# A split-fp16 product transposed by DMA in place of TensorE, and loops written out, in a gated two-layer kernel

## The chip, the cores and the metric

The kernel runs on one core of a Trainium2 chip. The metric is the device time of one execution in microseconds (us); the text compares medians of several runs. The profile is one execution, recorded by the hardware profiler. Engines are named as in the profile: PE is TensorE's matrix multiply, PEld its weight load, DVE is VectorE, ACT is ScalarE, POOL is GpSimd, SP is SyncE, which here only issues DMAs.

## The reference

There are 2048 tokens `x` of 512 numbers. Two layers follow each other. The first sends each token through the expert that its token id names (four experts, each one 512x512 matrix `W`, used for all three products of the layer); the second is a low-rank mixture of eight experts, of which each token takes its best two:

```python
# layer 1, per token with its expert e (Wg = Wu = Wd = ctx_2048):
h  = layernorm(x)
g  = silu(h @ Wg[e].T);  u = h @ Wu[e].T
x  = x + tanh(g_xattn) * ((g * u) @ Wd[e].T)
# layer 2, E = 8 experts of rank R = 16, top K = 2:
h2 = layernorm(x)
gates = softmax(h2 @ Wr + br + bonus);  top2 = top_k(gates, 2)
hid = relu(h2 @ Wd + bd);  eo = hid @ Wu + bu
x  = x + tanh(g_ffn) * sum_e(weight_e * eo_e)
```

Since `Wg` is `Wu`, the kernel computes one product `a` and forms `silu(a) * a` from it.

## The kernel before

**Tiles and pairs.** The tokens are sorted by expert, by gathers, into 16 tiles of 128 tokens. A tile that holds tokens of two experts is worked on once for each, so there are 19 (tile, expert) pairs. One step `i` of the program works on several pairs at once, as a software pipeline; each engine has its own list of instructions in an order written out by hand, and semaphores join them.

**Split products.** Each fp32 factor is split into two fp16 numbers, a high part and a low part, and a product is three matmuls (high by high, high by low, low by high) for each of four 128-deep slices: 12 matmuls (`split_product`, L603 to L605).

**A pair's way.** For pair `k`: ACT normalizes the tile (`h`, L824), PE transposes it (`ps_hT`), ACT and DVE split that into `hT_hi` (L810) and `hT_lo` (L1074), PE forms the first product `ps_a`, ACT takes `silu` (L805), DVE forms `prod` (L1068). In the next step PE transposes `prod` (four 128x128 fp32 transposes into PSUM, `ps_pT`, L624), ACT copies the high part `pT_hi` (L783), DVE subtracts it and leaves the low part `pT_lo` (L1104), PE forms the second product `ps_y`, and DVE adds it to the tile (L1086).

**A tile's way in layer 2.** When all pairs of a tile are added, DVE takes statistics (L1095, L1099), POOL the reciprocal root (`ve`, `rs`, `mrs`, L456 to L458), ACT normalizes (`h`, L796), PE transposes (`ps_h2T`, L685), ACT and DVE split (`h2T_hi` L815, `h2T_lo` L1110), PE forms the gates and hidden values (`ps_hid`), DVE finds the best two, ACT takes their `tanh` (`half_tanh`, L801), DVE forms the weights (`w`, L1169) and the weighted hidden values, PE transposes those (`ps_wT`) and forms the low-rank product (`ps_o`), and DVE adds it (L1117). POOL scatters the finished tile to its place.

**Order on the engines.** In a steady step DVE runs: best two, `wtT_lo`, `gwT`, `pT_lo` of the pair before, `w` and the weighting, `prod`, `hT_lo`, `h2T_lo`, the addition of the low-rank product, the addition of the second product of the pair before, statistics, hidden values. ACT runs: `pT_hi`, `wtT_hi`, `gwT`, `h` of layer 2, `tanh`, `silu`, `hT_hi`, `h2T_hi`, `h` of layer 1 for the pair after the next. PE runs: the hidden product, the four transposes of `prod`, the first product, the low-rank product, the transposes of `h`, those of layer 2's `h`, the second product of the pair before, the transposes of the weights.

**Start.** In the first steps ACT also squares and converts the expert weights and those of layer 2 (`square_sums`, `high_parts`, `ffn_squares`, L740 to L766), between the parts of the steps.

**Loops.** `pipeline` joins steps that do the same work into a loop whose body holds two steps: PE for steps 8 to 17, ACT for 8 to 13 and 15 to 16, DVE for 9 to 12 and 14 to 17. Step 13 is written out on DVE and POOL's work is written out throughout. In a loop the index is in a register; DVE clears a cell (`gate`, L1049) ahead of some instructions there, which takes their waits. SP counts arrived gathers into one semaphore (`x_in`), which a loop can wait for.

## Time and profile before

| what | value |
|---|---|
| median of 3 runs | 203.54 us (202.56 to 203.68) |
| span of the profiled execution | 201.4 us |
| busy on PE, share of the span | 175.0 us, 87% |
| busy on DVE | 155.7 us, 77% |
| busy on ACT | 111.9 us, 56% |
| busy on POOL | 99.7 us, 50% |
| mean DMA rate over the span | 67 GB/s |

The profiled execution's own time is its span, 201.4 us, and what lies around it; the median of the runs is 2.1 us above the span. Busy shares are means over the whole program, in which the start (weights are loaded, squared, split and transposed), the steady steps, and the end differ. A steady step takes a little over 8 us, and its limits are read from the timeline of each engine, not from the shares. A time ahead of an instruction's name is its start, counted from the span's start; the number behind it is its duration; instructions of one engine are pipelined, so the next one can start before the duration is over.

### The profile page before, as it was taken

The page shows a single profiled execution, that of the slowest core. Times are in us where ns is not written, and L with a number is a line of the kernel's source. Part 1 is how long each engine was busy: PE and PEld are TensorE (multiplying, and loading weights), DVE is VectorE, ACT ScalarE, POOL GpSimd, SP SyncE. Part 2 cuts the span into 40 slices and gives each one's busy share as a digit, 9 for nine tenths or more (in the row PEclk, how much of TensorE's full clock was granted, in tenths as well). Part 3 has the DMA queues.
Part 4 walks back from the last instruction along what each step waited for, and adds up shares of the span by engine and source line. Part 5 has one row for each costly group of instructions (what it writes and reads, how often), then busy time and mean ns, then how long its engine had stood idle before and what let it go on. Part 6 is the DMA issues. An engine that isn't in the chain of part 4 may idle for free.

```text
span 201.4 us, 4382 instructions
## 1 busy us (share of the span) xinstructions
PE 175.0 (87%) x1074; PEld 104.0 (52%) x1075; DVE 155.7 (77%) x523; ACT 111.9 (56%) x224; POOL 99.7 (50%) x246
## 2 busy tenths in 40 slices
PE   1576896999997989999999999999999999976560
PEld 1564463655553656656656556655665655534310
DVE  4859696697768799889888998797877878678640
ACT  2596599884287166473665726547265561545200
POOL 4478846427246366375553735516244162445641
PEclk9999999999999999999999999999999999999955
DMA  5947572101210201203101011011010100101121
GB/s 135 370 163 231 205 216 69 52 5 20 86 55 0 52 0 52 59 0 104 55 0 54 0 52 52 2 52 52 0 54 0 52 20 33 52 0 55 52 104 52
DMA packets 6784, 13.43 MB, mean 67 GB/s; under 512 B 2392, under 2 KB 2520, under 8 KB 6768
## 3 DMA queue, kind: packets, MB, share of 16 engines
q0 software_dynamic: 2560, 8.39, 12.6%
q1 hardware_dynamic: 4208, 4.86, 7.3%
q8 instruction: 6, 0.10, 0.2%
q14 instruction: 10, 0.08, 0.2%
HBM read 9.06 MB, written 4.19 MB: 66 GB/s over the span
## 4 chain that ended last, share of the span: by engine, by line
PE 44%; issue 18%; POOL 10%; DVE 9%; DMA 7%; ACT 4%; DVEq 3%; SPq 2%; POOLq 1%; ACTq 0%
PE ps_y L603 6%; PE ps_y L605 6%; PE ps_y L604 6%; PE ps_a L603 4%; PE ps_a L605 4%; PE ps_a L604 4%; DMA xs<-in_x_dram,rows_of 4%; ACT h L796 3%; POOL rs L457 3%; PE ps_h2T L685 2%; PE ps_pT L624 2%; DMA bu_nat<-in_L_ffn_bu_dram 2%; POOL hot_slot L432 2%; PE ps_hT L677 2%; POOL xs L439 2%
## 5 line engine op out<-in xcount | busy, mean ns | idle before, releaser
L456 POOL TENSOR_SCALAR ve<-mv 128x1 f32<-128x1 f32 x32 | 7.7, 239 | 62.6 <-DVE mv L1099 51.8
L796 ACT ACTIVATE h<-xs,mrs,rs 128x512 f32<-128x512 f32 (+1 forms) x16 | 21.1, 1317 | 22.4 <-POOL mrs L458 22.4
L783 ACT ACTIVATE pT_hi<-ps_pT 128x512 f16<-128x512 f32 x19 | 11.3, 595 | 36.0 <-PE ps_pT L624 36.0
L603 PE MATMUL ps_y<-w_hi,pT_hi 128*128 x76 | 28.8, 379 | 2.3 <-DVE w_lo L952 1.5
L603 PE MATMUL ps_a<-w_hi,hT_hi 128*128 x76 | 29.1, 382 | 0.7 <-DVE hT_lo L1074 0.6
L604 PE MATMUL ps_a<-w_lo,hT_hi 128*128 x76 | 29.1, 382 | 0.0
L605 PE MATMUL ps_a<-w_hi,hT_lo 128*128 x76 | 29.0, 381 | 0.0
L604 PE MATMUL ps_y<-w_lo,pT_hi 128*128 x76 | 28.8, 379 | 0.0
L605 PE MATMUL ps_y<-w_hi,pT_lo 128*128 x76 | 28.8, 379 | 0.0
L1086 DVE SCALAR_TENSOR_TENSOR xs<-ps_y,y_t,xs 128x512 f32 x19 | 14.3, 750 | 10.2 <-PE ps_y L605 7.7
L529 POOL DMA_INDIRECT out_dram<-xs,rows_of x16 | 17.3, 1083 | 5.9 <-DVE xs L1117 3.5
L457 POOL TENSOR_TENSOR rs<-ve,neg_half 128x1 f32<-128x1 f32 x32 | 18.9, 592 | 2.7
L439 POOL DMA_INDIRECT xs<-in_x_dram,rows_of x16 | 17.0, 1064 | 3.7 <-issue 2.9
L824 ACT ACTIVATE h<-xs,mrs,rs 128x512 f32 (+1 forms) x19 | 15.6, 820 | 4.3 <-POOL mrs L458 3.8
L1068 DVE SCALAR_TENSOR_TENSOR prod<-ps_a,prod_bits,silu 128x512 f32<-128x512 f32 x19 | 14.1, 744 | 1.6 <-ACT silu L805 1.6
L805 ACT ACTIVATE silu<-ps_a,inv_bits 128x512 f32<-128x512 f32 x19 | 12.8, 676 | 4.2 <-PE ps_a L605 4.2
L685 PE MATMUL ps_h2T<-ident,h 128*128 128x128 f32 x64 | 10.2, 281 | 4.2 <-ACT h L796 4.1
L1104 DVE TENSOR_TENSOR pT_lo<-ps_pT,pT_hi 128x512 f16<-128x512 f32 x19 | 13.1, 689 | 0.7 <-ACT pT_hi L783 0.3
L1117 DVE SCALAR_TENSOR_TENSOR xs<-ps_o,out_coef,xs 128x512 f32<-128x512 f32 (+1 forms) x16 | 11.9, 742 | 2.0 <-PE ps_o L645 2.0
L1074 DVE TENSOR_TENSOR hT_lo<-ps_hT,hT_hi 128x512 f16<-128x512 f32 x19 | 12.9, 680 | 0.3 <-ACT hT_hi L810 0.3
L740 ACT ACTIVATE sq_act<-w_nat 128x512 f32<-128x512 f32 x16 | 10.1, 634 | 5.4 <-DMA w_nat<-in_ctx_dram 5.0
L632 PE MATMUL ps_hid<-w_in_hi,h2T_hi 128*128 128x136 f16 x64 | 12.1, 223 | 0.6 <-DVE h2T_lo L1110 0.4
(209 smaller groups left out, 424.0 us busy)
## 6 DMA issues: line engine op xcount, KB each, us to landing
w_nat<-in_ctx_dram SPq DMA_DIRECT2D x4, 1024.0 KB, 7.9
xs<-in_x_dram,rows_of POOLq DMA_INDIRECT x16, 3.6
wd_nat<-in_L_ffn_Wd_dram SPq DMA_DIRECT2D x1, 256.0 KB
wu_nat<-in_L_ffn_Wu_dram SPq DMA_DIRECT2D x1, 256.0 KB
out_dram<-xs,rows_of POOLq DMA_INDIRECT x16, 2.9
...
tok_i<-in_itok_BxS_dram SPq DMA_DIRECT2D x1, 8.0 KB, 1.8
```

The lines of the kernel that those rows point to most:

```text
L439: g.indirect_dma_start(out=xs[:, t, :], out_offset=None, in_=x_rows[:, :], in_offset=bass.IndirectOffsetOnAxis(ap=rows_of[:, t:t + 1], axi ...
L457: then(g.tensor_tensor(rs[:, n, k:k + 1], ve[:, n, k:k + 1], neg_half[:, :], ALU.pow))
L529: g.indirect_dma_start(out=out_rows[:, :], out_offset=bass.IndirectOffsetOnAxis(ap=rows_of[:, k:k + 1], axis=0), in_=x1[:, k, :], in_offse ...
L603: mm(ps[:, :], lhs_hi[:, kc, :], hi, start=(kc == 0), stop=False)
L604: mm(ps[:, :], lhs_hi[:, kc, :], lo, start=False, stop=False)
L605: last = mm(ps[:, :], lhs_lo[:, kc, :], hi, start=False, stop=(kc == KC - 1))
L685: last = tr(ps_h2T[:, c, :], h2[:, c, :], ident[:, :])
L796: a(h2[:, :, :], x1[:, col(k), :].rearrange("p o (q c) -> p c (o q)", c=KC), ACT.Identity, bias=mrs[:, 1, col(k)], scale=rs[:, 1, col(k)]) ...
L824: a(h[:, :], flat(xs[:, col(tile), :]), ACT.Identity, bias=mrs[:, 0, col(tile)], scale=rs[:, 0, col(tile)]).then_inc(normed1, 1)
L1068: v.scalar_tensor_tensor(prod[:, :], ps_a[:, :], prod_t[:, col(k)], silu[:, :], ALU.mult, ALU.mult).then_inc(prod_done, 1)
L1086: v.scalar_tensor_tensor(flat(x1[:, col(tile), :]), ps_y[:, :], y_t[:, col(k)], flat(xs[:, col(source), :]), ALU.mult, ALU.add).then_inc(x ...
L1104: v.tensor_tensor(pT_lo[:, :, :], ps_pT[:, :, :], pT_hi[:, :, :], ALU.subtract).then_inc(pT_lo_done, 1)
```

## The change

PE no longer transposes `prod`. ACT copies `prod`'s high part (`p_hi`, from SBUF) and DVE subtracts it and leaves the low part (`p_low`), both side by side in a tile `p_split` with two buffers; SP issues one DMA per pair that transposes the two parts (128 x 1024 fp16 numbers, 256 KB) into `pT`, also of two buffers. The second product waits for that DMA. `p_hi` of pair `i` stands on ACT behind `h2T_hi` and ahead of layer 1's `h`, and `p_low` of pair `i` on DVE behind `h2T_lo` and ahead of the addition of the low-rank product, both in step `i`, where `pT_hi` and `pT_lo` of pair `i` stood in step `i + 1`. All loops are written out; `gate` and `x_in` are gone.

```diff
-                sp.sem_inc(x_in, 1)
...
+            for k in range(NP):
+                sp.wait_ge(p_hi_done, k + 1)
+                sp.wait_ge(p_lo_done, k + 1)
+                if k >= 2:
+                    sp.wait_ge(y_done, k - 1)
+                sp.dma_start_transpose(pT[:, k % 2, :, :, :].rearrange("p s c q -> p (s c) q"),
+                                       p_split[:, k % 2, :, :].rearrange("p s d -> p (s d)"))\
+                  .then_inc(pT_in[k % 2], 16)
             sp.wait_ge(s_scatter, 16 * T)
...
             def second_product(k, e):
-                pe.wait_ge(pT_lo_done, k + 1)
+                pe.wait_ge(pT_in[k % 2], 16 * (k // 2 + 1))
...
-                split_product(ps_y, pT_hi, pT_lo, e).then_inc(y_done, 1)
-
-            def transpose_product(k):
-
-                pe.wait_ge(prod_done, k + 1)
-                for c in range(KC):
-                    last = tr(ps_pT[:, c, :], prod[:, c * P:(c + 1) * P], ident[:, :])
-                last.then_inc(pT_done, 1)
+                split_product(ps_y, pT[:, k % 2, 0, :, :], pT[:, k % 2, 1, :, :], e).then_inc(y_done, 1)
...
@@ ACT, step @@
-                if some(NP, -1, i0):
-                    k = i - 1
-                    act.wait_ge(pT_done, k + 1)
-                    wait_last(act, y_done, k)
-                    a(pT_hi[:, :, :], ps_pT[:, :, :], ACT.Copy).then_inc(pT_hi_done, 1)
...
+                if some(NP, 0, i0):
+                    k = i
+                    act.wait_ge(prod_done, k + 1)
+                    if k >= 2:
+                        act.wait_ge(pT_in[k % 2], 16 * (k // 2))
+                    a(p_split[:, k % 2, 0, :], prod[:, :], ACT.Copy).then_inc(p_hi_done, 1)
...
@@ DVE @@
             def product(k):
                 dve.wait_ge(silu_done, k + 1)
+                wait_last(dve, p_lo_done, k)
...
-            def pT_low(k):
-
-                dve.wait_ge(pT_hi_done, k + 1)
-                v.tensor_tensor(pT_lo[:, :, :], ps_pT[:, :, :], pT_hi[:, :, :],
-                                ALU.subtract).then_inc(pT_lo_done, 1)
+            def p_low(k):
+
+                dve.wait_ge(p_hi_done, k + 1)
+                if k >= 2:
+                    dve.wait_ge(pT_in[k % 2], 16 * (k // 2))
+                v.tensor_tensor(p_split[:, k % 2, 1, :], prod[:, :], p_split[:, k % 2, 0, :],
+                                ALU.subtract).then_inc(p_lo_done, 1)
...
-                if some(NP, -1, i0) and not ending:
-                    pT_low(i - 1)
...
                 if some(T, -2 - LATE, i0) and not draining:
                     h2T_low(i - 2 - LATE)
+                if some(NP, 0, i0):
+                    p_low(i)
                 if some(T, -4 - LATE, i0) and not draining:
                     add_low_rank(i - 4 - LATE)
...
-        def pipeline(eng, step, first, pairs, tiles):
...
-                    with eng.Fori(0, (last - first) // 2) as n:
-                        step(n * 2 + (first + odd), first)
-                        step(n * 2 + (first + odd + 1), first)
...
+        def pipeline(step, first, pairs, tiles):
+
+            for i in range(first, max(NP - min(pairs), T - min(tiles))):
+                step(i, i)
```

On DVE, in a full step that is written out before (`xs` in the last row is the addition of the low-rank product), the program before has:

```order
L1150 TENSOR_TENSOR wtT_lo<-ps_wT,wtT_hi 128x128 [waits wtT_hi_done]
L1151 TENSOR_TENSOR gwT<-ps_wT,gwT 8x128
L1104 TENSOR_TENSOR pT_lo<-ps_pT,pT_hi 128x512 [waits pT_hi_done]
L1169 SCALAR_TENSOR_TENSOR w<-half_dif,half_tanh,half_sum 128x8 [waits wtT_done,mix_done,tanh_done]
L1172 SCALAR_TENSOR_TENSOR weighted<-hid,w 128x128 [waits w8_done]
L1176 TENSOR_SCALAR w_rep<-w,ffn_bits 128x3x8
L1068 SCALAR_TENSOR_TENSOR prod<-ps_a,prod_bits,silu 128x512 [waits silu_done]
L1074 TENSOR_TENSOR hT_lo<-ps_hT,hT_hi 128x512 [waits hT_hi_done]
L1110 TENSOR_TENSOR h2T_lo<-ps_h2T,h2T_hi 128x512 [waits h2T_hi_done]
L1117 SCALAR_TENSOR_TENSOR xs<-ps_o,out_coef,xs 128x512 [waits o_mm]
```

The changed program has there (`p_split` is written by `p_low`; its lines are numbered anew):

```order
L1115 TENSOR_TENSOR wtT_lo<-ps_wT,wtT_hi 128x128 [waits wtT_hi_done]
L1116 TENSOR_TENSOR gwT<-ps_wT,gwT 8x128
L1132 SCALAR_TENSOR_TENSOR w<-half_dif,half_tanh,half_sum 128x8 [waits wtT_done,mix_done,tanh_done]
L1135 SCALAR_TENSOR_TENSOR weighted<-hid,w 128x128 [waits w8_done]
L1139 TENSOR_SCALAR w_rep<-w,ffn_bits 128x3x8
L1035 SCALAR_TENSOR_TENSOR prod<-ps_a,prod_bits,silu 128x512 [waits p_lo_done,silu_done]
L1041 TENSOR_TENSOR hT_lo<-ps_hT,hT_hi 128x512 [waits hT_hi_done]
L1077 TENSOR_TENSOR h2T_lo<-ps_h2T,h2T_hi 128x512 [waits h2T_hi_done]
L1071 TENSOR_TENSOR p_split<-prod,p_split 128x512 [waits pT_in0,p_hi_done]
L1084 SCALAR_TENSOR_TENSOR xs<-ps_o,out_coef,xs 128x512 [waits o_mm]
```

The subtraction for the low part moved from ahead of `w`, for the pair before, to behind `h2T_lo`, for the pair of this step.

On ACT, at the start of the program, after the first product of pair 1, the program before has (the row of `h` is layer 1's for tile 3, then come the squares of the weights; `pT_hi` of pair 1 follows behind all squares):

```order
L805 ACTIVATE silu<-ps_a,inv_bits 128x512 [waits a_done]
L810 ACTIVATE hT_hi<-ps_hT 128x512 [waits a_done,hT_done]
L820 TENSOR_LOAD pair_tile_i
L820 ISA x2
L824 ISA [waits hT_done,rstd1]
L824 ACTIVATE h<-xs,mrs,rs 128x512
L740 ACTIVATE sq_act,row_sq<-w_nat 128x512 [waits s_sq,s_wload3]
```

The changed program has there:

```order
L774 ACTIVATE silu<-ps_a,inv_bits 128x512 [waits a_done]
L779 ACTIVATE hT_hi<-ps_hT 128x512 [waits a_done,hT_done]
L790 ACTIVATE p_split<-prod 128x512 [waits prod_done]
L795 TENSOR_LOAD pair_tile_i
L795 ISA x2
L799 ISA [waits hT_done,rstd1]
L799 ACTIVATE h<-xs,mrs,rs 128x512
L714 ACTIVATE sq_act,row_sq<-w_nat 128x512 [waits s_sq,s_wload3]
```

The copy of the high part, which waits for `prod` of pair 1, stands ahead of `h` and of the squares, and there is none behind the squares.

## Rows read from the trace of the kernel before

**Rows 1.** Windows: us, busy of PE, PEld, DVE, ACT, POOL, PEclk, DMA share, GB/s

```profile
83.87:92.16 8.29, 8.29 (x58) 5.00 (x55) 7.43 (x26) 4.73 (x9) 5.40 (x13) 1.00 0.14 42
...
134.70:168.22 33.52, 33.49 (x219) 19.98 (x217) 26.50 (x84) 18.24 (x35) 13.29 (x36) 1.00 0.08 32
```

**Rows 2.** Timeline of PE: start us, us, line, operation [idle before, releaser]

```profile
72.06 0.38 PE L603 MATMUL ps_y<-w_hi,pT_hi 128*128 x1
...
75.58 0.60 PE L624 MATMUL ps_pT<-ident,prod 128*128 128x128 f32 x4
76.02 0.38 PE L603 MATMUL ps_a<-w_hi,hT_hi 128*128 x1
...
168.22 0.60 PE L624 MATMUL ps_pT<-ident,prod 128*128 128x128 f32 x4
```

**Rows 3.** Timeline of DVE, the written-out step 13

```profile
130.55 0.23 DVE L1169 SCALAR_TENSOR_TENSOR w<-half_dif,half_tanh,half_sum 128x8 f32<-128x8 f32 x1 [1.19 <-ACT half_tanh L801]
...
131.17 0.73 DVE L1068 SCALAR_TENSOR_TENSOR prod<-ps_a,prod_bits,silu 128x512 f32<-128x512 f32 x1
...
132.42 0.68 DVE L1110 TENSOR_TENSOR h2T_lo<-ps_h2T,h2T_hi 128x512 f16<-128x512 f32 x1
133.02 0.74 DVE L1117 SCALAR_TENSOR_TENSOR xs<-ps_o,out_coef,xs 128x512 f32<-128x512 f32 x1
133.94 0.75 DVE L1086 SCALAR_TENSOR_TENSOR xs<-ps_y,y_t,xs 128x512 f32 x1 [0.18 <-issue]
...
136.99 0.69 DVE L1104 TENSOR_TENSOR pT_lo<-ps_pT,pT_hi 128x512 f16<-128x512 f32 x1
138.60 0.23 DVE L1169 SCALAR_TENSOR_TENSOR w<-half_dif,half_tanh,half_sum 128x8 f32<-128x8 f32 x1 [0.91 <-ACT half_tanh L801]
```

**Rows 4.** Timeline of ACT, the same step

```profile
131.47 0.59 ACT L815 ACTIVATE h2T_hi<-ps_h2T 128x512 f16<-128x512 f32 x1
...
137.06 1.32 ACT L796 ACTIVATE h<-xs,mrs,rs 128x512 f32<-128x512 f32 x1 [0.79 <-POOL mrs L458]
```

**Rows 5.** Timeline of DVE, two additions of the second product

```profile
75.08 0.75 DVE L1086 SCALAR_TENSOR_TENSOR xs<-ps_y,y_t,xs 128x512 f32 x1 [0.29 <-PE ps_y L605]
...
142.52 0.75 DVE L1086 SCALAR_TENSOR_TENSOR xs<-ps_y,y_t,xs 128x512 f32 x1 [0.62 <-PE ps_y L605]
```

**Rows 6.** Timeline of DVE, a subtraction with both inputs in SBUF

```profile
68.54 0.74 DVE L1041 SCALAR_TENSOR_TENSOR wu_lo<-wu_nat,ffn_bits,wu_hi 128x512 f16<-128x512 f32 x1
```

**Rows 7.** Costliest groups: busy us, mean ns of one | idle before, releaser

```profile
L740 ACT ACTIVATE sq_act<-w_nat 128x512 f32<-128x512 f32 x16 | 10.1, 634 | 5.4 <-DMA w_nat<-in_ctx_dram 5.0
```

**Rows 8.** DMA issues: KB each, median us from issue to landing

```profile
w_nat<-in_ctx_dram SPq DMA_DIRECT2D x4, 1024.0 KB, 7.9
xs<-in_x_dram,rows_of POOLq DMA_INDIRECT x16, 3.6
...
tok_i<-in_itok_BxS_dram SPq DMA_DIRECT2D x1, 8.0 KB, 1.8
```

**Rows 9.** Timelines of ACT and DVE at the start, in order of time

```profile
34.08 0.86 ACT L824 ACTIVATE h<-xs,mrs,rs 128x512 f32 x1
...
35.42 0.72 DVE L1068 SCALAR_TENSOR_TENSOR prod<-ps_a,prod_bits,silu 128x512 f32<-128x512 f32 x1
...
39.83 0.60 ACT L783 ACTIVATE pT_hi<-ps_pT 128x512 f16<-128x512 f32 x1 [0.42 <-PE ps_pT L624]
40.32 0.68 ACT L752 ACTIVATE w_hi<-ps_h2T,scale_w 128x512 f16<-128x512 f32 x1
...
44.73 0.75 DVE L1068 SCALAR_TENSOR_TENSOR prod<-ps_a,prod_bits,silu 128x512 f32<-128x512 f32 x1 [0.20 <-ACT silu L805]
```

**Rows 10.** Timelines of PE and DVE, second product of pairs 2 and 18, `prod` of 18

```profile
49.37 0.38 PE L603 MATMUL ps_y<-w_hi,pT_hi 128*128 x1
...
173.43 0.73 DVE L1068 SCALAR_TENSOR_TENSOR prod<-ps_a,prod_bits,silu 128x512 f32<-128x512 f32 x1
...
178.05 0.39 PE L603 MATMUL ps_y<-w_hi,pT_hi 128*128 x1 [0.79 <-DVE pT_lo L1104]
```

More of the change, by code:

```diff
@@ L192, in bass_flamingo_gated_kernel @@
         prod = sb("prod", [P, D])
-        pT_hi = sb("pT_hi", [P, KC, P], fp16)
-        pT_lo = sb("pT_lo", [P, KC, P], fp16)
+        p_split = sb("p_split", [P, 2, 2, D], fp16)
+        pT = sb("pT", [P, 2, 2, KC, P], fp16)
         h2 = sb("h2", [P, KC, P])
@@ L275, in bass_flamingo_gated_kernel @@
         prod_done = sem("prod_done")
[L276 to L278 removed]
+        p_hi_done = sem("p_hi_done")
+        p_lo_done = sem("p_lo_done")
+        pT_in = [sem("pT_in0"), sem("pT_in1")]
         y_done = sem("y_done")
@@ L311, in some @@
             return 0 <= i + off < n
-        def pipeline(eng, step, first, pairs, tiles):
-            def work(i):
-                return ([(some(NP, off, i), i + off == 0) for off in pairs]
-                        + [(some(T, off, i), i + off == 0) for off in tiles])
-            end = max(NP - min(pairs), T - min(tiles))
-            while first < end:
-                last = first + 1
-                while last < end and work(last) == work(first):
-                    last += 1
-                if last == first + 1:
-                    step(first, first)
-                else:
-                    odd = (last - first) % 2
-                    if odd:
-                        step(first, first)
-                    with eng.Fori(0, (last - first) // 2) as n:
-                        step(n * 2 + (first + odd), first)
-                        step(n * 2 + (first + odd + 1), first)
-                first = last
+        def pipeline(step, first, pairs, tiles):
+            for i in range(first, max(NP - min(pairs), T - min(tiles))):
+                step(i, i)
         def col(k):
@@ new lines, in _ @@
+            sp.wait_ge(s_gather[0], 16)
+            load_weights(3)
+            sp.wait_ge(s_gather[1], 16)
+            sp.dma_start(gates_in[:, 0:1], g_xattn.rearrange("(a n) -> a n", a=1).to_broadcast([P, 1])).then_inc(s_gates_in, 16)
+            sp.dma_start(gates_in[:, 1:2], g_ffn.rearrange("(a n) -> a n", a=1).to_broadcast([P, 1])).then_inc(s_gates_in, 16)
+            sp.wait_ge(s_gather[AHEAD - 1], 16)
+            sp.dma_start(b_in[:, 0:ER], bd.rearrange("(a e) r -> a (e r)", a=1).to_broadcast([P, ER])).then_inc(s_small, 16)
@@ new lines, in _ @@
+            sp.dma_start(b_in[:, ER:HC], br.rearrange("(a e) -> a e", a=1).to_broadcast([P, EF])).then_inc(s_small, 16)
+            sp.dma_start(wr_nat[:, :, :], Wr.rearrange("(p c) e -> p c e", c=KC)).then_inc(s_small, 16)
+            sp.dma_start(wd_nat[:, :, :, :], Wd.rearrange("e (p c) r -> p e (c r)", c=KC)).then_inc(s_small, 16)
+            sp.dma_start(wu_nat[:, :], Wu.rearrange("e r d -> (e r) d")).then_inc(s_small, 16)
+            sp.wait_ge(s_const, 2)
+            for n in range(3):
+                sp.dma_start(bu_nat[n * Q:n * Q + EF, :], bu[:, :]).then_inc(s_small, 16)
@@ L727, in _ @@
             pe.wait_ge(s_ffn_w, 2)
-            pipeline(pe, step, 7, (-1, 0, 1), (-2 - LATE, -3 - LATE, -4 - LATE))
+            pipeline(step, 7, (-1, 0, 1), (-2 - LATE, -3 - LATE, -4 - LATE))
         @block.scalar
@@ L856, in _ @@
             ffn_high_parts()
-            pipeline(act, step, 5, (-1, 0, 1, 2), (2, -2 - LATE, -3 - LATE, -4 - LATE))
+            pipeline(step, 5, (-1, 0, 1, 2), (2, -2 - LATE, -3 - LATE, -4 - LATE))
         @block.vector
@@ L1217, in _ @@
             hT_low(1)
+            p_low(0)
             statistics1(3)
@@ L1235, in _ @@
             ffn_out_low_parts()
-            pipeline(dve, step, 6, (-1, 0, 1), (3, -1 - LATE, -2 - LATE, -3 - LATE, -4 - LATE))
+            pipeline(step, 6, (-1, 0, 1), (3, -1 - LATE, -2 - LATE, -3 - LATE, -4 - LATE))
 _INS = ['x', 'itok_BxS_13_99985', 'ctx_2048', 'g_xattn', 'g_ffn', 'L0_ffn_Wr', 'L0_ffn_br',
```

38 lines of the change are left out of this document (1 added, 37 removed).

## The prediction

> **What bounds the kernel now.** I read four views in this order: the window table, the timeline of VectorE over one step, the timelines of ScalarE and TensorE beside it, and the start and end of the program.
>
> The window table shows that TensorE has no gap in the middle of the program: 8.29 us busy in a window of 8.29 us, which is one step, and 33.49 of 33.52 us over four later ones [rows 1]. The granted clock there is 1.00, which is the 2.4 GHz level. Four transposes of `prod` stand in each step: they begin at 75.58 and the next product begins at 76.02, so they cost 0.44 us of TensorE's step [rows 2]. From the first of these (75.58) to the last one in the steady part (168.22) there are 11 steps, 92.64 us, or 8.42 us each.
>
> VectorE's timeline shows a second loop that is as long. In the one steady step whose instructions are written out already (step 13), the operation `w` begins at 130.55 and again at 138.60: 8.05 us [rows 3]. Between them follow, without idle time, `prod`, `hT_lo`, `h2T_lo`, the addition of the low-rank product (L1117), the addition of the second product (L1086) and the statistics. These release GpSimd's reciprocal root, which releases ScalarE's `h` at 137.06; the `tanh` stands behind `h` on ScalarE, and `w` waits for that `tanh` (idle 1.19 us before the first `w`, 0.91 us before the second) [rows 3, 4]. So a microsecond put anywhere between `w` and the statistics comes out at the next `w`. A microsecond put between the statistics and the next `w` doesn't: VectorE idles there anyway. `pT_lo` stands just there, at 136.99, before that idle time. Two loops thus bind at once, TensorE's 8.29 and this one's 8.05 and more; the looped steps are longer than either number because each waits for the other now and then, as the addition that waited 0.62 us for `ps_y` at 142.52 [rows 5].
>
> **The change, part by part.**
>
> *TensorE* loses the four transposes: 8.29 − 0.44 = 7.85 us a step. Alone this pays only as far as the other loop lets it.
>
> *VectorE* does as many subtractions as before, but `p_low` moves from the covered place (136.99) to the place between `h2T_lo` and the addition of the low-rank product, that is between 132.42 and 133.02, inside the chain. A subtraction of this size takes 0.60 us from start to start where its first input lies in PSUM (`h2T_lo`, 132.42 to 133.02) [rows 3]; the nearest row with both tensor inputs in SBUF took 0.74 us (`wu_lo`) [rows 6]. I take 0.65, nearer to the first since it is the same operation. The loop becomes 8.05 + 0.60 to 8.05 + 0.74, that is 8.65 to 8.79; I take 8.70, above TensorE's 7.85, so this loop sets the step. Over 11 steps: 95.7 − 92.6 = **+3.1 us**. In the two steps ahead of that stretch VectorE still waits for `ps_y` (0.29 us at 75.08 [rows 5]), and 0.60 − 0.29 = **+0.3 us** is left.
>
> *ScalarE* copies `p_hi` from SBUF in place of `pT_hi` from PSUM: 0.63 us by the squares of the same size from SBUF [rows 7]. In a steady step `prod` ends at 131.90, so `p_hi` would run from there to 132.53, after `h2T_hi` (begun 131.47, 0.59 us), and be done before `p_low` gets its turn at 133.02 [rows 3, 4]: cost nothing, hidden beside `hT_lo` and `h2T_lo`. If `prod` came later against these two, `p_low` would wait for it and the step would grow by that much.
>
> *The transfer.* One DMA per pair moves 256 KB from SBUF to SBUF and transposes it. No row of before shows such a transfer. Its landing is bounded by 1.8 us (an 8 KB load on the same queue) and 7.9 us (1 MB on the same queue); the nearest row in size is the gather of 256 KB, 3.6 us [rows 8]. I take 3.6. Below 1.8 nothing speaks for it, since that is the least that this queue shows for a far smaller load. In a steady step there is room: from `w` to `p_low`'s end 133.02 − 130.55 + 0.70 = 3.17; then the landing; from the first matmul of the second product to its addition 75.08 − 72.06 = 3.02 [rows 2, 5]; from that addition to the next `w` 138.60 − 133.94 = 4.66 [rows 3]. Together 10.85 us plus the landing have to fit in two steps, 17.4 us: hidden up to a landing of 6.5 us. Beyond, a step is half of the sum, 0.5 us more for each us.
>
> The Trainium skill gives prices for this transfer. "DMA: Bandwidth & Descriptors", section "Latency and other measured facts", has 261 GB/s for a transposing DMA and about 2 us of fixed cost: 1.0 + 2.0 = 3.0 us (estimate), inside the room worked out above. No run here shows it yet.
>
> *The start.* There no low-rank product fills the steps yet, and ScalarE, which squares and converts the weights, is the narrow place. `p_hi` of pair 1 stands ahead of the first normalization of tile 3 (L824), which began at 34.08; but `prod` of pair 1 ends only at 35.42 + 0.72 = 36.14 [rows 9]. That normalization can begin at 36.14 + 0.63 = 36.77, 2.7 us later. Of this, `pT_hi` and its wait go (0.42 idle and 0.49 to the next start, at 39.83), so `w_hi` of 40.32 is 1.8 late. `prod` of pair 2 (44.73) can be late by 0 to 1.8; I take 1.1, as ScalarE has some idle time between: 45.83. Then 0.75 + 0.63 + 0.69 to the end of `p_low` and 3.6 to land: 51.5, where the second product began at 49.37 [rows 10]; +2.1. TensorE works 0.44 less behind it: **+1.7 us**.
>
> *The end.* `prod` of the last pair begins at 173.43; + 0.73 + 0.63 + 0.69 + 3.6 = 179.1 against the second product at 178.05 [rows 10]: **+1.0 us**.
>
> *Loops written out* takes away branches and registers. The written-out step of 8.05 from which I started has that already, so it is in the 8.70.
>
> Sum, on the span of the profiled execution: 201.4 + 1.7 + 0.3 + 3.1 + 1.0 = 207.5 us. The median of the runs, 203.54, is 2.1 us above that span, so the time is 207.5 + 2.1 = **209.6 us**.
>
> With a landing of 1.8 us and `p_low` at 0.60, start and end cost nothing and the middle 2.5: 206.3. With a landing of 6 us and 0.74: start 4.1, two steps 0.3, middle 4.1, end 3.4, which gives 215.4. So this case's own range is 206 to 215.5.
>
> **The rivals.**
>
> *The transfer comes late in every step.* The place is the second product's wait for the DMA; it decides from a landing of 6.5 us on. For it: the 1 MB row of the same queue, 7.9 us, and that no row shows what transposing adds. Against it: 256 KB is a quarter of that row, and the gather of as much took 3.6 [rows 8]. At 7.9 us a step is (10.85 + 7.9) / 2 = 9.38: middle 103.1 − 92.6 = +10.5, two steps before it 0.3 + 2 × 0.68 = +1.7, start 1.7 + 4.3 = +6.0, end 1.0 + 4.3 = +5.3, together +23.5: 227.0 us.
>
> A rule of the Trainium skill speaks for this rival. "VectorE: DVE Perf Modes", sections "The three transpose paths" and "Rules for kernel authors", has 390 ns for a 128x128 transpose on TensorE and 1309 ns by DMA, and advises TensorE wherever the result may go to PSUM. Eight one after the other would be 10.5 us (estimate), still later than this rival has it. The trace has 0.11 us for a transpose on TensorE in this stream (0.44 for four), less than the page; its DMA figure no run here shows.
>
> *Faster: `p_low` falls into idle time.* If the step is bound by TensorE and the written-out step is an exception, VectorE has 0.6 us to spare and the step is 7.85: 11 × 7.85 = 86.4, −6.3; with start and end 201.4 − 6.3 + 1.7 + 1.0 = 197.8, time 199.9 us. For it: the 0.62 us that the addition waited for `ps_y` [rows 5]. Against it: in the written-out step VectorE waited for `tanh` alone, and that wait is the loop itself [rows 3].
>
> *No change.* A landing near 1.8 us takes start and end away, and half of `p_low` is hidden by what the looped steps waited for TensorE, so that the step stays at 8.42: 201.4 + 0.3 + 2.1 = 203.8.
>
> **How the numbers follow.** The forecast gets 0.62, the late transfer 0.20, faster 0.12, no change 0.06. What this kernel's measurement can tell from no change is about 0.5%, 202.5 to 204.6 us. The first two cases are slower: 0.82. The late transfer holds landings from 6.5 us, 215 us and more, to 7.9, 227 us, and beyond; the range goes to 224 and takes in most of it, and down to 203.5, which takes in half of no change. The likeliest case's own range is 206 to 215.5.
>
> **What would show it.** In the steady steps of the changed kernel: from `w` to `w` 8.65 to 8.79 us; `p_low` directly behind `h2T_lo`, and the addition of the second product behind it without a wait for `ps_y`; TensorE idle by some 0.8 us a step, mostly before `ps_h2T`; the landing of `pT` between 3 and 5 us, and no wait of `ps_y` for it there. At the start the normalization of tile 3 begins near 36.8, and the second product of pair 2 waits for the DMA, as that of pair 18 does at the end. I am wrong if `w` to `w` is below 8.4 (then VectorE had the room), or if `ps_y` waits for the DMA in every step (then the landing is above 6.5 us).

## The result and the profile after

| | median | runs | ratio to before (95%) |
|---|---|---|---|
| before | 203.31 us | 202.56 to 203.68 | |
| changed | 210.40 us | 207.67 to 212.24 | 1.030 (1.025 to 1.036) |

The ratios here and below leave out single executions that took over 1.5% longer than the fastest of their kernel (here the one of 212.24 us, and in experiment 8 one of 590.6 us whose cause isn't known); the medians have them in.

The profiled execution of the changed kernel took 210.76 us with a span of 209.0, 7.6 us more than the 201.4 of before. Its page, part 1 (busy time, share of the span, instructions of each engine):

```profile
PE 172.3 (82%) x998; PEld 96.4 (46%) x998; DVE 155.6 (74%) x442; ACT 115.0 (55%) x223; POOL 100.4 (48%) x246
```

VectorE's busy time is what it was (155.6 after 155.7 us): nothing was added there, one thing was moved, and the 80 short clears of `gate` are gone. I read next the landing of the transfer in the DMA issues of the page (the last number, in us), then VectorE's timeline over one steady step:

```profile
pT<-p_split SPq DMA_TRANSPOSE x19, 3.6
```

```profile
153.78 0.23 DVE L1132 SCALAR_TENSOR_TENSOR w<-half_dif,half_tanh,half_sum 128x8 f32<-128x8 f32 x1 [1.69 <-ACT half_tanh L770]
...
154.25 0.23 DVE L1139 TENSOR_SCALAR w_rep<-w,ffn_bits 128x24 f32<-128x24 f32 x1
154.51 0.75 DVE L1035 SCALAR_TENSOR_TENSOR prod<-ps_a,prod_bits,silu 128x512 f32<-128x512 f32 x1
155.17 0.68 DVE L1041 TENSOR_TENSOR hT_lo<-ps_hT,hT_hi 128x512 f16<-128x512 f32 x1
155.77 0.68 DVE L1077 TENSOR_TENSOR h2T_lo<-ps_h2T,h2T_hi 128x512 f16<-128x512 f32 x1
156.37 0.68 DVE L1071 TENSOR_TENSOR p_split<-prod,p_split 128x512 f16<-128x512 f32 x1
156.97 0.74 DVE L1084 SCALAR_TENSOR_TENSOR xs<-ps_o,out_coef,xs 128x512 f32<-128x512 f32 x1
157.63 0.74 DVE L1053 SCALAR_TENSOR_TENSOR xs<-ps_y,y_t,xs 128x512 f32 x1
...
162.27 0.23 DVE L1132 SCALAR_TENSOR_TENSOR w<-half_dif,half_tanh,half_sum 128x8 f32<-128x8 f32 x1 [1.70 <-ACT half_tanh L770]
```

This answers to [rows 3]. From `w` to `w` it is 8.49 us. `p_split` stands between `h2T_lo` and the addition of the low-rank product and costs 0.60 from start to start; the idle time before `w`, where `pT_lo` used to lie, is 1.69 us in place of 0.91. The twelve steps from `w` to `w` were not alike: 8.24 for the first, which has no low-rank addition yet, 8.69 for the second, then 8.48 to 8.50 for six, 8.64 for three and 9.01 for one. In the table of windows the steady part, from the second product of pair 5 to that of pair 17, is:

```profile
76.37:179.57 103.20, 98.40 (x598) 53.62 (x596) 84.16 (x229) 58.16 (x108) 48.86 (x131) 1.00 0.32 65
```

TensorE is no longer full there (98.40 of 103.20 us), where before it was in the windows of [rows 1]. Twelve steps took 103.20 us, 8.60 each; before they took 101.08 (72.06 to 173.14).

TensorE's timeline at the start and the end (first matmul of a pair's second product, and of layer 2's transposes), answering to [rows 10]:

```profile
51.66 0.39 PE L588 MATMUL ps_y<-w_hi,pT 128*128 x1 [1.22 <-DMA pT<-p_split]
...
57.42 0.38 PE L588 MATMUL ps_y<-w_hi,pT 128*128 x1
...
65.86 0.66 PE L659 MATMUL ps_h2T<-ident,h 128*128 128x128 f32 x4 [2.66 <-ACT h L765]
...
66.79 0.38 PE L590 MATMUL ps_y<-w_hi,pT 128*128 x1
...
67.35 0.63 PE L589 MATMUL ps_y<-w_lo,pT 128*128 x1
...
185.35 0.39 PE L588 MATMUL ps_y<-w_hi,pT 128*128 x1 [2.09 <-DMA pT<-p_split]
```

The idle 2.66 us (65.86) stand ahead of the transposes that come just before the second product of pair 4. Of 19 second products only two, those of pairs 2 and 18, waited for the DMA. Behind the idle 2.66 us a matmul takes 0.63 in place of 0.38 us: the granted clock fell. The windows of these two places, with the clock in the column behind POOL:

```profile
67.00:70.63 3.63, 3.63 (x10) 1.31 (x9) 1.96 (x4) 1.69 (x3) 0.73 (x1) 0.53 0.34 99
...
186.74:189.30 2.56, 2.56 (x7) 0.99 (x6) 0.00 (x0) 0.85 (x2) 1.68 (x4) 0.50 0.03 11
```

So the 7.6 us lie as follows, by the start of the second product in both traces: up to pair 3 +1.82 (57.42 against 55.60), pairs 3 to 5 +2.49 (18.95 against 16.46), the steady part +2.12, the last pair +0.87 (5.78 against 4.91), and +0.30 behind it (23.65 against 23.35).

### The profile page after: what moved, and what is told of

Read it like the earlier page. It is cut to its first block, busy times and chain, and to the rows that moved or that the text cites. A ratio compares the mean times of both kernels' runs of the same rounds, so it can differ in the third digit from the quotient of the medians.

```text
span 209.0 us, 4000 instructions
## 1 busy us (share of the span) xinstructions
PE 172.3 (82%) x998; PEld 96.4 (46%) x998; DVE 155.6 (74%) x442; ACT 115.0 (55%) x223; POOL 100.4 (48%) x246
## 4 chain that ended last, share of the span: by engine, by line
DVE 28%; issue 19%; POOL 10%; PE 7%; ACT 6%; DVEq 6%; DMA 3%; POOLq 1%; SPq 0%; ACTq 0%
DVE xs L1053 5%; DVE prod L1035 5%; DVE st L1061 5%; POOL rs L442 4%; DVEq L1047 3%; DMA pT<-p_split 3%; DVE h2T_lo L1077 3%; PE ps_y L588 2%; POOL mrs L443 2%; PE ps_y L589 2%; PE ps_y L590 2%; ACT half_tanh L770 2%; POOL ve L441 2%; DVE w L1132 2%; DVE w_rep L1139 1%
## 5 line engine op out<-in xcount | busy, mean ns | idle before, releaser
L765 ACT ACTIVATE h<-xs,mrs,rs 128x512 f32<-128x512 f32 x16 | 21.0, 1313 | 50.5 <-POOL mrs L443 50.5
L588 PE MATMUL ps_y<-w_hi,pT 128*128 x76 | 30.0, 395 | 4.6 <-DMA pT<-p_split 3.3
L588 PE MATMUL ps_a<-w_hi,hT_hi 128*128 x76 | 29.6, 389 | 1.2 <-DVE hT_lo L1041 1.2
L589 PE MATMUL ps_y<-w_lo,pT 128*128 x76 | 30.1, 396 | 0.0
L590 PE MATMUL ps_y<-w_hi,pT 128*128 x76 | 30.0, 395 | 0.0
L589 PE MATMUL ps_a<-w_lo,hT_hi 128*128 x76 | 29.6, 389 | 0.0
L1132 DVE SCALAR_TENSOR_TENSOR w<-half_dif,half_tanh,half_sum 128x8 f32<-128x8 f32 x16 | 3.7, 229 | 16.6 <-ACT half_tanh L770 14.9
L659 PE MATMUL ps_h2T<-ident,h 128*128 128x128 f32 x64 | 10.8, 292 | 5.1 <-ACT h L765 5.1
L1071 DVE TENSOR_TENSOR p_split<-prod,p_split 128x512 f16<-128x512 f32 x19 | 13.0, 686 | 0.6
L790 ACT ACTIVATE p_split<-prod 128x512 f16<-128x512 f32 x19 | 12.0, 630 | 2.6 <-DVE prod L1035 2.6
L588 PEld LDWEIGHTS ps_y<-w_hi,pT 128*128 128x128 f16 x76 | 7.6, 100 | 12.4 <-issue 6.1
```

What stands on the lines that cost most here:

```text
L588: mm(ps[:, :], lhs_hi[:, kc, :], hi, start=(kc == 0), stop=False)
L589: mm(ps[:, :], lhs_hi[:, kc, :], lo, start=False, stop=False)
L590: last = mm(ps[:, :], lhs_lo[:, kc, :], hi, start=False, stop=(kc == KC - 1))
L765: a(h2[:, :, :], x1[:, col(k), :].rearrange("p o (q c) -> p c (o q)", c=KC), ACT.Identity, bias=mrs[:, 1, col(k)], scale=rs[:, 1, col(k)]) ...
L1071: v.tensor_tensor(p_split[:, k % 2, 1, :], prod[:, :], p_split[:, k % 2, 0, :], ALU.subtract).then_inc(p_lo_done, 1)
```

## The experiments

Each ratio is to the kernel before, which ran beside it. Theory 1 is the prediction's: the transfer is hidden in the steady steps, and `p_low`'s place in VectorE's chain sets them. (Only the expectation of experiment 1 uses the name for something else, a cost of the loops.) Where one number is given for a step, it is typical of the later ones of the twelve.

**1. `loops_alone`.** The kernel before with its loops written out; nothing else (`gate` and `x_in` stay).

```diff
-                    with eng.Fori(0, (last - first) // 2) as n:
-                        step(n * 2 + (first + odd), first)
...
+            for n in range(first, max(NP - min(pairs), T - min(tiles))):
+                step(n, n)
```

> The kernel before with its loops written out and nothing else changed; TensorE still transposes the product. Theory 1 (loops cost, because the written-out step of before took 8.05 us and the looped ones 8.2 to 8.7): the steady step comes to TensorE's 8.29, 11 x (8.42 - 8.29) = 1.4 us faster or a little more, 200.5 to 202.3 us. Rival (a loop costs nothing, the steps vary for other reasons): 203.3 within 0.5.

Measured: 201.12 us, ratio 0.991 (0.987 to 0.995), as its first theory had it and not its rival. The steady part in its windows, again 12 steps:

```profile
71.79:170.96 99.17, 99.17 (x647) 59.81 (x645) 84.16 (x278) 56.47 (x108) 49.75 (x132) 1.00 0.10 36
```

TensorE is busy in all of it, 8.26 us a step. The change thus held a gain of 2.2 us (the loops) and a loss of 9.3 (the transfer with what was moved for it). The forecast had put the first at nothing, since its 8.70 was built on a written-out step.

**2. `twin_transfer`.** A second transposing DMA of the same parts ahead of the one that counts.

```diff
-                sp.dma_start_transpose(pT[:, k % 2, :, :, :].rearrange("p s c q -> p (s c) q"),
+                for dst in (pT_twin, pT):
+                    sp.dma_start_transpose(dst[:, k % 2, :, :, :].rearrange("p s c q -> p (s c) q"),
...
-                pe.wait_ge(pT_in[k % 2], 16 * (k // 2 + 1))
+                pe.wait_ge(pT_in[k % 2], 32 * (k // 2 + 1))
```

> The changed kernel, with a second transposing DMA of the same parts into an unused tile ahead of the one that counts; the second product and the reuse of the buffers wait for both. Landing from the copies' end goes from 3.6 to between 4.8 us (one issue of 1.23 us more) and 7.2 us. Theory 1 (in the steady steps VectorE's chain sets the pace, and a landing is hidden up to 6.5 us): the steady step stays at 8.5 to 8.65, and only the start and the end each grow by what the landing grows, 1.2 to 2.9 us each where it stays under 6.5: 212.5 to 216 us. Rival (the transfer sets the step): each step grows by half of the landing's growth, 12 x 0.6 to 12 x 1.8 us more, 219 us and above.

Measured: 216.19 us, ratio 1.056 (1.047 to 1.066). Windows of the steady part, and the last pair on TensorE's timeline:

```profile
80.08:183.25 103.17, 98.49 (x598) 53.63 (x596) 84.17 (x229) 58.17 (x108) 48.85 (x131) 1.00 0.47 95
```

```profile
190.46 0.60 PE L590 MATMUL ps_y<-w_hi,pT 128*128 x1 [3.53 <-DMA pT<-p_split]
```

Twice the transposing, 95 in place of 65 GB/s, and the 12 steps took 103.17 us against 103.20. The last pair took 7.21 against 5.78. In the steady steps the longer landing costs nothing, at the ends it is paid. Theory 1 holds there; its rival, a step set by the transfer, is out. The total lies 0.2 us above the top of the expected range, since the start lost 3.7 us (second product of pair 5 at 80.08 in place of 76.37) and not 1.2 to 2.9: pair 2 waited 3.78 us for the DMA here, and the granted clock behind that was 0.60 for 3.5 us.

**3. `clock_held`.** Filler transposes of the identity into the free bank, in two idle stretches of TensorE (the other one has 16, ahead of the last second product).

```diff
+                if i == 4:
+                    keep_busy(20)
```

> The changed kernel, with 20 transposes of the identity into an unused bank ahead of the first transposes of layer 2 (step 4, where TensorE was idle for 2.66 us) and 16 ahead of the last second product (2.09 us idle). Theory 3 (these idle stretches let the granted clock fall to half for about 3.6 us behind them): the clock stays at 1.00 there, the second product of pair 4 runs in 2.6 us in place of 4.3 and that of pair 18 in 2.6 in place of 3.95, and the time is 2 to 3.3 us shorter, 207 to 208.4 us. Rival (the next wait takes it back, since the fillers delay nothing but gain nothing): 210.4 within 0.7.

Measured: 210.06 us, ratio 1.032 (1.026 to 1.039): no gain that can be told, so theory 3's 207 to 208.4 us is missed and its rival holds. In the profiled execution (212.95 us, the longest of the four and 2.9 above the median, so it is read for its pieces only) the clock stayed at 1.00 where the filler was, and pairs 3 to 5 took 16.53 us, as before the change. But there the wait of pair 2 for the DMA was 2.43 us, and the clock fell behind that:

```profile
52.73:56.50 3.77, 3.77 (x12) 1.49 (x13) 0.07 (x1) 0.24 (x1) 0.42 (x1) 0.63 0.65 139
...
62.35:70.46 8.11, 6.28 (x34) 3.24 (x32) 4.24 (x12) 4.54 (x8) 2.60 (x7) 1.00 0.36 66
```

That the fall at pair 4 is worth 1.7 us is seen in the pieces; that removing it makes the kernel faster by as much is not shown. Nor does the fall come in every execution: in the one profiled for experiment 5 TensorE was idle for 2.41 us at the same place, the clock stayed at 1.00, and pairs 4 to 5 took 8.41 us in place of 10.01:

```profile
65.67 0.66 PE L659 MATMUL ps_h2T<-ident,h 128*128 128x128 f32 x4 [2.41 <-ACT h L765]
```

**4. `two_parts_late_low`.** A DMA for each part, the high part's matmuls first, `p_low` behind the statistics.

```diff
+                sp.dma_start_transpose(pT[:, k % 2, 0, :, :], p_split[:, k % 2, 0, :]).then_inc(pT_in[k % 2], 16)
+                sp.wait_ge(p_lo_done, k + 1)
+                sp.dma_start_transpose(pT[:, k % 2, 1, :, :], p_split[:, k % 2, 1, :]).then_inc(pT_lo_in[k % 2], 16)
...
                         statistics2(i - 1 - LATE)
+                if some(NP, 0, i0) and behind:
+                    p_low(i)
```

> The changed kernel with two edits: a DMA for each part (the high part's is issued as soon as the high part is there), the second product taking its eight matmuls on the high part first; and p_low in the steady steps behind the statistics of layer 2, outside VectorE's chain. Theory 1 (p_low's place in the chain is what costs in the steady steps): the step goes from 8.56 to between 7.9 and 8.1, 12 steps give 5.5 to 8 us, the end 1 to 1.7 us: 201 to 204 us. Rival (the transfer's landing sets the step, wherever p_low stands): the second product waits for the low part in each step, the step stays at 8.4 or more: 208 to 211 us.

Measured: 207.40 us, ratio 1.019 (1.013 to 1.025), steady step 8.36. Both expectations are missed: the time lies between them, the step is above theory 1's 7.9 to 8.1, and no second product of the steady part waited for the DMA, which was the rival's reason. (The last pair gained 1.4 us, and the start lost 1.9: second product of pair 5 at 78.23.) VectorE's and GpSimd's timelines:

```profile
158.47 0.18 DVE L1072 BATCH_NORM_AGGREGATE mv<-st 128x2 f32<-128x6 f32 x1
158.56 0.67 DVE L1079 TENSOR_TENSOR p_split<-prod,p_split 128x512 f16<-128x512 f32 x1
...
158.75 0.58 POOL L441 TENSOR_SCALAR ve<-mv 128x1 f32<-128x1 f32 x1 [4.14 <-DVE mv L1072]
```

`ve` takes 0.58 us beside `p_low`, and 0.24 in the changed kernel, where no operation on two SBUF inputs runs beside it (the group's mean there is 239 ns). `ve` is in the chain, so the place behind the statistics is not free either: 0.60 saved, 0.34 given back, and another 0.12 stands between the two additions (0.78 from start to start, 0.66 in the changed kernel). The Trainium skill has this in "SBUF — State Buffer", section "SBUF: two separate sides": a VectorE operation with two SBUF inputs and a GpSimd operation that reads SBUF exclude each other for a whole instruction. The two rows agree with it: `p_low` runs to 159.23 and `ve` to 159.33.

**5. `low_rank_behind`.** `p_low` stays; the addition of the low-rank product goes behind the statistics.

```diff
-                if some(T, -4 - LATE, i0) and not draining:
+                if some(T, -4 - LATE, i0) and ending:
                     add_low_rank(i - 4 - LATE)
...
                         statistics2(i - 1 - LATE)
+                if some(T, -4 - LATE, i0) and not draining and not ending:
+                    add_low_rank(i - 4 - LATE)
```

> The changed kernel; the addition of the low-rank product stands on VectorE behind the statistics of layer 2 (ahead of the hidden values) in place of between p_low and the addition of the second product. p_low stays where it is. Theory 1 (whatever lies between w and the statistics sets the step): the chain gets 0.66 to 0.8 shorter, from 8.5 to 8.65 to 7.85 to 7.9, where TensorE's own 7.85 takes over: 12 steps give 7.5 to 9 us, 201.5 to 203 us. Rival (an operation behind the statistics holds up GpSimd, whose first operation took 0.58 in place of 0.24 us in the kernel with the late p_low, and so the chain): step about 8.2, 205.5 us.

Measured: 207.78 us, ratio 1.023 (1.019 to 1.028), step 8.40: neither theory 1's 201.5 to 203 nor the rival's 205.5. `ve` took 0.24 (this operation has one input in PSUM), so the rival's reason is out, and yet the step stayed above 7.9. The timelines of TensorE and VectorE, in order of time, show why:

```profile
151.52 0.38 PE L588 MATMUL ps_y<-w_hi,pT 128*128 x1
...
154.54 0.75 DVE L1053 SCALAR_TENSOR_TENSOR xs<-ps_y,y_t,xs 128x512 f32 x1 [0.46 <-PE ps_y L590]
...
158.17 0.39 PE L620 MATMUL ps_o<-wu_hi,wtT_hi 128*128 128x512 f16 x1 [0.38 <-DVE gwT L1116]
...
159.93 0.38 PE L588 MATMUL ps_y<-w_hi,pT 128*128 x1
```

`gwT` stands on VectorE behind the moved addition, and TensorE waits for it ahead of the low-rank product. So another loop closes here: from the second product to its addition 3.02 us, from there over the statistics, the moved addition, the hidden values and the best two to `gwT` and the low-rank product 3.63, from that to the next second product 1.76, together 8.41. The addition left the chain over `w`, but it lies in this loop.

**6. `first_pairs_on_pe`.** Pairs 0 to 4 and 18 are transposed by TensorE as before, the others by DMA.

```diff
+        by_dma = [5 <= k <= 17 for k in range(NP)]
```

> The changed kernel; pairs 0 to 4 and 18 are transposed by TensorE as in the kernel before, pairs 5 to 17 by DMA. Theory 1 (at the start the copy on ScalarE and the landing are exposed, 4.3 us up to the second product of pair 5, and 0.9 at the last pair): 5 us less, 204.5 to 206 us. Rival (the lateness at the start is the clock's, whose dips come anyway): less than 2 us gained, 208.4 us or more.

Measured: 204.80 us, ratio 1.009 (1.005 to 1.012): 5.6 us less than the changed kernel, as theory 1 had it; the rival, a dip of the clock that comes anyway, is out. Start and end are the loops-alone kernel's again (second product of pair 3 at 55.55 and 55.33; last pair 4.91 and 4.90 us). What is left over 201.12 is 3.7 us, and the steady part alone is 102.97 against 99.17:

```profile
72.08:175.05 102.97, 98.38 (x599) 53.55 (x596) 84.22 (x229) 58.13 (x108) 49.34 (x131) 1.00 0.29 65
```

**7. `first_pairs_on_pe_low_rank_behind`.** Both edits.

> Both edits, pairs 0 to 4 and 18 on TensorE and the addition of the low-rank product behind the statistics. If the two terms are independent: 210.4 - 5 - 8 = 197 us, 196 to 199, below the loops written out alone (201.1). If one of the rivals holds: 200 to 203 us.

Measured: 204.17 us, ratio 1.006 (1.003 to 1.010), step 8.40: neither 196 to 199 nor 200 to 203, since edit 5 is worth little (0.6 us here).

**8. `places_first`.** The loads of a tile's place ahead of `p_low`.

```diff
+                if some(NP, -1, i0) and not ending:
+                    where = place(i - 1)
                 if some(NP, 0, i0):
                     p_low(i)
...
-                        add_y(i - 1, *place(i - 1))
+                        add_y(i - 1, *where)
```

> The changed kernel; the two loads of a tile's place into registers stand ahead of p_low on VectorE in place of behind it. In step 4 the addition of the second product waited 1.22 us for nothing but its own issue, since the loads could begin only behind p_low. Theory 4 (the loads behind p_low make step 4 longer by 0.8 us, TensorE's idle time behind it grows, and the clock falls): y of pair 4 comes 0.8 earlier, and with the clock held y of pair 5 another 1.7: 208 to 209.6 us. Rival (something else sets that wait): 210.4 within 0.5.

Measured: 213.52 us, ratio 1.048 (1.042 to 1.054): slower than the changed kernel, and outside both expectations. Its timelines of VectorE:

```profile
60.22 0.74 DVE L1053 SCALAR_TENSOR_TENSOR xs<-ps_y,y_t,xs 128x512 f32 x1
...
166.35 0.69 DVE L1071 TENSOR_TENSOR p_split<-prod,p_split 128x512 f16<-128x512 f32 x1 [0.44 <-issue]
```

In step 4 the addition no longer waits (in the changed kernel it began at 61.27, after 1.22 us of idle time put down to its own issue), and the second product of pair 4 came 8.35 us behind that of pair 3 in place of 8.94. That half of theory 4 holds. But the clock fell all the same (pair 4 to 5 took 10.03), and in the steady steps the loads now idle VectorE for 0.44 us inside the chain: step 8.76, later 9.03. From the first addition to the second, though, it was 0.66 to 0.67 in every one of them.

**9. `spare_subtraction`.** The loops written out alone, and one subtraction of `p_low`'s size on unused tiles in `p_low`'s place.

```diff
+                if some(NP, 0, i0):
+                    dve.wait_ge(spare_done, 2 + i - 1)
+                    v.tensor_tensor(spare_lo[:, :], spare[:, :], spare_hi[:, :],
+                                    ALU.subtract).then_inc(spare_done, 1)
                 if some(T, -4 - LATE, i0) and not draining:
                     add_low_rank(i - 4 - LATE)
```

> The loops written out alone (201.1 us, steady step 8.29), plus one subtraction per step on VectorE of the size of p_low, from two unused SBUF tiles into a third, between h2T_lo and the addition of the low-rank product. TensorE still transposes the product and no transposing DMA runs. Theory 1 (p_low's place in VectorE's chain is the whole cost in the steady steps): the step goes to 8.5 to 8.65 as in the changed kernel, 12 steps give 2.5 to 4.3 us: 203.6 to 205.4 us. Rival (VectorE has room there, and what makes the changed kernel's steady step longer belongs to the transfer): 201.1 within 0.7.

Measured: 202.15 us, ratio 0.997 (0.994 to 0.999); 1.0 us over `loops_alone`, between theory and rival. Its VectorE timeline:

```profile
138.18 0.23 DVE L1169 TENSOR_SCALAR w_rep<-w,ffn_bits 128x24 f32<-128x24 f32 x1
138.32 0.73 DVE L1061 SCALAR_TENSOR_TENSOR prod<-ps_a,prod_bits,silu 128x512 f32<-128x512 f32 x1
...
140.17 0.68 DVE L1179 TENSOR_TENSOR spare_lo<-spare,spare_hi 128x512 f16<-128x512 f32 x1
140.77 0.74 DVE L1110 SCALAR_TENSOR_TENSOR xs<-ps_o,out_coef,xs 128x512 f32<-128x512 f32 x1
141.43 0.74 DVE L1079 SCALAR_TENSOR_TENSOR xs<-ps_y,y_t,xs 128x512 f32 x1
```

The step is 8.36, not 8.5 to 8.65. The subtraction puts 0.60 in, but the second addition now begins 0.66 behind the first, where in [rows 3] it began 0.92 behind. In `loops_alone` it was 1.17, part of it a wait for `ps_y`:

```profile
148.24 0.74 DVE L1104 SCALAR_TENSOR_TENSOR xs<-ps_o,out_coef,xs 128x512 f32<-128x512 f32 x1
149.41 0.75 DVE L1073 SCALAR_TENSOR_TENSOR xs<-ps_y,y_t,xs 128x512 f32 x1 [0.43 <-PE ps_y L592]
```

VectorE had 0.51 us of room in each step there, so that its own chain is 8.29 - 0.51 = 7.78 long, and 0.60 more makes 8.38. Twelve steps took 100.23 us against 99.17: of the 3.8 us by which the steady part of experiment 6 lies above `loops_alone`, a subtraction in this place accounts for 1.1.

Against the changed kernel's 8.49 the step lacks 0.13, of which 0.12 stand at one place: `prod` begins 0.14 behind `w_rep` here and 0.26 there, and 0.08 behind the end of `silu` here and 0.19 there, where it waits for `p_low` of the pair before as well. In the changed kernel's longer steps another 0.15 (8.64) or 0.52 (9.01) stands between the two additions; that is the loads', since it is gone where they stand ahead of `p_low` (experiment 8). What makes the 0.12 wasn't tried. The spare subtraction waits for no other engine and `p_low` waits for ScalarE's copy, so the rest may belong to `p_low`'s waits or to the transfer; that doubling the transfer changed nothing (experiment 2) speaks for the waits.

**10. `from_pair_2`.** As 6, but pairs 2 to 17 by DMA (`by_dma = [2 <= k <= 17 ...]`).

> The changed kernel; pairs 0, 1 and 18 are transposed by TensorE as in the kernel before, pairs 2 to 17 by DMA. What goes at the start is ScalarE's wait for the product of pair 1; the landing of pair 2 stays exposed. Theory 1: prod of pair 2 begins at 44.7 in place of 46, its second product at 44.73 + 0.75 + 0.63 + 0.69 + 3.6 = 50.4 in place of 51.66, still waiting for the DMA; with the last pair's 0.9 this is 2.1 us less: 208.3, between 207.3 and 209 us. Rival (the copy on ScalarE is not what is late): the second product of pair 2 stays at 51.7 and only the last pair's 0.9 goes: 209.5 us or more.

Measured: 206.19 us, ratio 1.014 (1.009 to 1.019). TensorE and VectorE at the start:

```profile
44.98 0.75 DVE L1074 SCALAR_TENSOR_TENSOR prod<-ps_a,prod_bits,silu 128x512 f32<-128x512 f32 x1 [0.22 <-ACT silu L810]
```

```profile
50.48 0.39 PE L603 MATMUL ps_y<-w_hi,pT 128*128 x1 [0.70 <-DMA pT<-p_split]
```

Both places come where theory 1 has them (44.7 and 50.4), so the new route of pairs 0 and 1 is what made pair 2 late, and the rows of ScalarE further down place it at the copy. The total gained 4.2 us, twice the 2.1 expected. The profiled execution (208.09) still had the fall of the clock at pair 4; what the faster ones had there isn't recorded.

**11. `weights_low_first`.** 7, with `wtT_lo` and `gwT` ahead of the moved addition.

> The kernel with pairs 0 to 4 and 18 on TensorE and the addition of the low-rank product behind the statistics (204.2 us, steady step 8.40), and wtT_lo and gwT on VectorE taken ahead of that addition in place of behind the hidden values and the best two: in the step of 8.40 TensorE waited 0.38 us for gwT ahead of the low-rank product. Theory 5 (that wait is the bound now): step 7.9 to 8.05, 12 steps give 4 to 6 us, 198 to 200.5 us, below the loops written out alone. Rival (the loop from the second product over the statistics, GpSimd and the normalization back to the transposes and the second product takes 8.4 whatever stands beside it): 204.2 within 0.7.

Measured: 208.69 us, ratio 1.029 (1.023 to 1.034), slower than 7 and outside both expectations: step 8.93. TensorE's timeline:

```profile
140.23 0.38 PE L647 MATMUL ps_o<-wu_hi,wtT_hi 128*128 128x512 f16 x1 [0.68 <-DVE xs L1133]
```

The wait for `gwT` is gone and the one for the bank stands in its place: the product may not start before the addition of the tile before has read `ps_o`.

**12. `two_banks_places_ahead`.** 7, with a second bank for the low-rank product and the loads of a place ahead of `w`.

> The kernel with pairs 0 to 4 and 18 on TensorE and the addition of the low-rank product behind the statistics (204.2 us, step 8.40), with two more edits: the low-rank product of every second tile goes to the bank that the transposes left free, so that it doesn't wait for the addition of the one before; and the loads of a tile's place stand ahead of w, where VectorE waits for the tanh, so that they don't lie between p_low and the addition of the second product. If TensorE's 0.44 us can be cashed in once nothing but its own work and the chain over the statistics is left: step 8.0, 12 x 0.4 = 5 us less, 199 us, below the loops written out alone (201.1). Rival (the loop second product, its addition, statistics, GpSimd, normalization, transposes, second product holds the step at 8.3): 202 to 203.5 us, not below it.

Measured: 207.49 us, ratio 1.021 (1.017 to 1.025), above both expectations. The late steps took 8.40, as without it, and TensorE waited for `gwT` again (0.37 us); the early ones took 8.87, where `w` waits 1.17 us for its own issue:

```profile
118.07 0.23 DVE L1196 SCALAR_TENSOR_TENSOR w<-half_dif,half_tanh,half_sum 128x8 f32<-128x8 f32 x1 [1.17 <-issue]
```

The second bank thus takes away the wait for the bank and leaves the loop of experiment 5. Experiment 11's order together with the second bank was not run; whether the step would then come down to TensorE's own work is open.

None of the runs with the transfer beats `loops_alone`. Only it and, by less, `spare_subtraction`, both of which leave the transposes on TensorE, beat both kernels.

## Why the prediction was right, and where not

The forecast was 209.6 us and slower; measured were 210.4. On the span it had +6.1 us and the trace shows +7.6. That the total came this near is in part luck: the steady part was forecast 1.0 us too long and the two steps ahead of it 2.2 too short. By its steps:

- **The transfer, hidden in the steady steps: right, and shown.** Landing taken as 3.6, measured 3.6 (3.0 to 4.3). Doubling it left 12 steps at 103.17 us (experiment 2). The figure of the Trainium skill that stood for the late transfer ("VectorE: DVE Perf Modes", section "The three transpose paths", 1309 ns for a 128x128 block by DMA) can't be multiplied by eight: eight blocks landed in 3.6 us. The advice of the Trainium skill (the same page, section "Rules for kernel authors"), TensorE where PSUM will do, is what `loops_alone` bears out, though the landing is only a part of why, at pairs 2 and 18.
- **The start, +1.7: right in size and place, +1.82.** ScalarE's timeline of the changed kernel has the steps one by one, answering to [rows 9]:

```profile
36.15 0.63 ACT L790 ACTIVATE p_split<-prod 128x512 f16<-128x512 f32 x1 [0.33 <-DVE prod L1035]
36.91 0.82 ACT L799 ACTIVATE h<-xs,mrs,rs 128x512 f32 x1
...
42.10 0.66 ACT L726 ACTIVATE w_hi<-ps_h2T,scale_w 128x512 f16<-128x512 f32 x1
```

The forecast had 36.77 for the normalization, 42.1 for `w_hi`, 45.83 for `prod` of pair 2 (45.64 measured) and 51.5 for its second product (51.66). Experiments 6 and 10 bear it out.

- **The two steps behind it, +0.3: the term that was mis-sized; +2.49.** It was reckoned from 0.29 us that an addition waited for `ps_y` at 75.08, which is that of pair 5, and taken once for two steps. The additions of pairs 3 and 4 waited 1.19 and 1.01 us before, so `p_low` itself had room there. The timelines of VectorE and TensorE before, in order of time:

```profile
58.62 0.75 DVE L1086 SCALAR_TENSOR_TENSOR xs<-ps_y,y_t,xs 128x512 f32 x1 [1.19 <-PE ps_y L605]
...
63.23 0.66 PE L685 MATMUL ps_h2T<-ident,h 128*128 128x128 f32 x4 [1.42 <-ACT h L796]
...
66.74 0.75 DVE L1086 SCALAR_TENSOR_TENSOR xs<-ps_y,y_t,xs 128x512 f32 x1 [1.01 <-PE ps_y L605]
```

Two things were missed. `p_low` stands ahead of the loads of the tile's place too, and in step 4 no low-rank addition covers those: the addition of the second product waited 1.22 us for its own issue, +0.82; in the changed kernel:

```profile
61.27 0.75 DVE L1053 SCALAR_TENSOR_TENSOR xs<-ps_y,y_t,xs 128x512 f32 x1 [1.22 <-issue]
```

So TensorE was idle for 2.66 us in place of 1.42, and the clock halved for the next 3.6 us, +1.67. The first is shown by experiment 8 (the wait gone, the step 0.6 shorter); of the second only the pieces are shown. The place alone doesn't do it: in experiment 9, too, a subtraction stands ahead of these loads, and its addition in step 4 waited for `ps_y` alone:

```profile
57.83 0.75 DVE L1079 SCALAR_TENSOR_TENSOR xs<-ps_y,y_t,xs 128x512 f32 x1 [0.54 <-PE ps_y L596]
```

What differs is that `p_low` waits for ScalarE's copy, which ended at 59.32; `p_low` began at 59.35. That the loads are held back by this wait is argued from the two traces, not tried.

- **The steady steps, 8.70: right in kind, a little too long.** 8.60 measured, below the 8.65 to 8.79 given. The term for 11 steps was +3.1; 12 steps gave +2.12. `p_low` costs its 0.60 as forecast, and no second addition of these steps waited for `ps_y`. But the 8.05 that I started from was no bare chain: the row of the second addition there has 0.18 us of idle time, which the prediction read as none, and 0.26 us that stood between the two additions vanished under `p_low` (experiment 9). The chain alone is 7.78; `p_low` makes it 8.38, and 0.11 to 0.63 came in elsewhere, the loads' part of it shown by experiment 8, the rest without a known cause. That this chain sets the step is borne out only in part: each time something was taken out of it (experiments 4 and 5), the step fell to 8.36 and 8.40 and not to 7.9, because the next wait stood close behind. TensorE's idle time is 0.40 us a step and not 0.8, and shows ahead of `ps_o` and not, as forecast, ahead of `ps_h2T`.
- **The end, +1.0: right, +0.87.** Behind it the second product of pair 18 ran in part at half clock (0.50), so that its addition came 4.42 us behind its start in place of 3.02, which was not forecast; of that +0.30 is left at the program's end.
- **Loops written out.** Putting them at nothing left the sum near but hid what the change was made of: 2.2 us gained and 9.3 lost, 5.6 of these at the first and last pairs (experiment 6) and 3.7 in the steady steps.
